# Macaron block on one core: FFN tiles turned by VectorE blocks and DMA instead of TensorE transposes, LayerNorm sums on ScalarE

## What is computed

```python
x = x + 0.5 * ffn(layernorm(x))
x = x + attention(layernorm(x))
x = x + 0.5 * ffn(layernorm(x))

def ffn(x):                       # T = 8192 tokens
    scores = sigmoid(x @ gate_w.T)
    idx = top_k(scores + gate_b, 4)
    w = scores[idx]; w = 2.5 * w / sum(w)       # comb: 16 weights a token, 12 of them zero
    y = sum over e of comb[:, e] * ((silu(g_e) * u_e) @ w2[e].T),  g_e, u_e = split(x @ w13[e].T)
    return y + the shared expert
```

## Time and profile before

| | us |
|---|---|
| median of 3 runs (833.62 to 835.65) | 834.15 |
| the profiled execution, whole | 834.31 |
| its span | 832.5 |
| TensorE busy | 819.8 (98%) |
| VectorE busy | 722.7 (87%) |
| ScalarE busy | 552.3 (66%) |
| GpSimd busy | 613.9 (74%) |

### The profile page before, as it was taken

How to read it: one execution, slowest core, us unless ns; L and a number is a source line. 1 busy time by engine, 2 the same in 40 slices (tenths; PEclk the granted TensorE clock), 3 DMA queues, 4 the chain that set the end, 5 groups by cost and what they waited for, 6 DMA issues and landing times.

```text
span 832.5 us, 16260 instructions
## 1 busy us (share of the span) xinstructions
PE 819.8 (98%) x4229; PEld 672.1 (81%) x4229; DVE 722.7 (87%) x2120; ACT 552.3 (66%) x1167; POOL 613.9 (74%) x559
## 2 busy tenths in 40 slices
PE   8899999999999999999999999999999999999998
PEld 7677777777777777899999989677777777777777
DVE  7989999999998987788888876799999999998886
ACT  5566666666666677776667666666666666666664
POOL 7767777777777688888888883476777777777664
PEclk9999999999999999999999999999999999999999
DMA  6787766666676633443333430555656655555553
GB/s 195 212 249 203 199 167 169 176 176 183 186 188 174 163 107 88 128 127 94 86 104 99 128 102 1 131 150 160 162 156 167 161 158 142 142 154 142 159 135 89
DMA packets 69376, 123.07 MB, mean 148 GB/s; under 512 B 8784, under 2 KB 19904, under 8 KB 69056
## 3 DMA queue, kind: packets, MB, share of 16 engines
q1 hardware_dynamic: 69312, 122.33, 54.7%
HBM read 104.28 MB, written 9.63 MB: 137 GB/s over the span
## 4 chain that ended last, share of the span: by engine, by line
PE 58%; DVE 3%; issue 1%; POOL 1%; DMA 1%; SPq 0%; ACT 0%; DVEq 0%; ACTq 0%; POOLq 0%
PE bank L1638 53%; PE bank L2009 4%; PE bank L1769 1%; DMA qkT<-comb_rows 1%; SPq L416 0%; DVE prob L1199 0%; POOL h_l L538 0%; DVE bank L1515 0%; PE bank L1746 0%; DVE xl L1482 0%; PE bank L1753 0%; DVE bank L1503 0%; POOL rstd L666 0%; DMA comb_rows<-combT 0%; DVE marked L1165 0%
## 5 line engine op out<-in xcount | busy, mean ns | idle before, releaser
L538 POOL TENSOR_TENSOR h_l<-probT,h_h 128x512 fp32r<-128x512 f32 x254 | 330.1, 1300 | 165.6 <-ACT h_h L760 164.7
L1638 PE MATMUL bank<-xh,w_h 128*128 128x512 f32 x545 | 223.4, 410 | 1.9 <-DVE prob L1199 1.7
L760 ACT ACTIVATE h_h<-probT 128x512 fp32r<-128x512 f32 (+1 forms) x285 | 178.7, 627 | 62.2 <-DVE probT L1209 59.5
L820 ACT ACTIVATE bank<-bank 128x512 f32<-128x512 f32 x252 | 146.8, 582 | 103.7 <-PE bank L1638 101.2
L1638 PE MATMUL bank<-xh,w_l 128*128 128x512 f32 x545 | 215.0, 395 | 0.0
L1638 PE MATMUL bank<-xl,w_h 128*128 128x512 f32 x545 | 214.8, 394 | 0.0
L1199 DVE TENSOR_TENSOR prob<-bank,qkT 128x512 f32<-128x512 f32 x252 | 172.9, 686 | 25.2 <-ACT bank L820 18.7
L1209 DVE TENSOR_TENSOR probT<-prob,bank 128x512 f32<-128x512 f32 x255 | 172.1, 675 | 15.0 <-POOL h_l L538 3.5
L1638 PEld LDWEIGHTS bank<-xh,w_h 128*128 128x128 f32 x545 | 103.2, 189 | 30.4 <-DVE prob L1199 3.5
L1638 PEld LDWEIGHTS bank<-xh,w_l 128*128 128x128 f32 x545 | 102.4, 188 | 23.8
L1638 PEld LDWEIGHTS bank<-xl,w_h 128*128 128x128 f32 x545 | 102.8, 189 | 19.3
(11 more groups left out here) (144 smaller groups left out, 1309.9 us busy)
## 6 DMA issues: line engine op xcount, KB each, us to landing
qkT<-comb_rows SPq DMA_DIRECT2D x190, 256.0 KB, 5.3
qkT<-comb_rows SPq DMA_DIRECT2D x124, 128.0 KB, 3.0
rows<-comb_rows SPq DMA_DIRECT2D x28, 512.0 KB, 7.2
stage<-stage SPq DMA_DIRECT2D x64, 128.0 KB, 2.4
X<-in_x SPq DMA_DIRECT2D x16, 256.0 KB, 7.4
stage<-in_x_t SPq DMA_DIRECT2D x16, 256.0 KB, 7.3
x_t<-stage SPq DMA_DIRECT2D x16, 256.0 KB, 2.0
out_x_t<-stage SPq DMA_DIRECT2D x15, 256.0 KB, 2.0
```

What stands on the lines that cost most here:

```text
L538: nc.gpsimd.tensor_tensor(lo, f, hi.bitcast(F32), ALU.subtract).then_inc(done, 1)
L760: return nc.scalar.activation(dst, src, ACT.Copy)
L820: nc.scalar.activation(bank[:, G_BANK[g], :], bank[:, G_BANK[g], :], ACT.Silu).then_inc(silu_done, 1)
L1638: return nc.tensor.matmul(dst, lhsT, rhs, start=start, stop=stop)
```

## The change

1. **Turning.** Token n * 128 + a * 32 + r of a tile now stands in column a * 128 + n * 32 + r. Then four 32x32 block transposes of VectorE and a DMA that moves partition groups give the full turn. In the first FFN VectorE turns each tile (`ffn_turn`, one 128x512 instruction), four DMAs write it to DRAM (`write_x1_rows`) and one DMA per sequence reads it back (`load_x1_rows`). In the second FFN VectorE turns the tokens of tile t + 4 (`turn_x2`), four DMAs write and one reads (`write_x2`, `load_x2`). `ffn_y`, `ffn_xT` and ScalarE's copies are gone. Four of the turns of the second FFN are made in the last batches of attention.
2. **Routing.** VectorE turns the logits and comb itself, in one 128x128 instruction each. The chain from logits to comb is spread over one more step of the tile.
3. **Statistics.** ScalarE sums them for tile T + 4 in steps 4 to 7 of tile T, in eight activations with an accumulator; VectorE's `ffn_stats` and `ffn_mv` stay at the start and in attention only.
4. **Loads.** `mask`, `cos` and `sin` are read at tiles 10 to 12 of the first FFN instead of at its start. The loops on SyncE and ScalarE over the FFN's tiles are written out.
5. **Scores.** Row 4's 640 columns are computed as two halves of 320, in six matmuls of 320 columns.

Core of the diff:

```diff
+            def ffn_means(T, Tx, q, part, base):
+                act.wait_ge(mv_done, ln_count(T - 1, base))
+                for n in (2 * part, 2 * part + 1):
+                    x = row_block(Tx, n) if base else raw_block(Tx, n)
+                    ins = nc.scalar.activation(unused[:, n, :, :], x, ACT.Identity, scale=MEAN_SCALE, accum_out=mv[...])
+            def ffn_vars(T, Tx, q, part, base):      # the same with ACT.Square, bias=mean, accum_out=mv[...]
...
-                    if base:
-                        if j == 0 and ahead:
-                            ffn_xT(T + 2, turn + (c + 2) // RING, (c + 2) % RING)
-                    elif j == PAIRS - 1 and not first:
-                        ffn_X(T - 1, T - 1)
+                    if j >= NB and j < PAIRS and (t is None or t + TURN_AHEAD < TILES):
+                        if j == NB and not base:
+                            act.wait_ge(x_next[q], 16 * (2 * turn + c // 2 + 1))
+                        (ffn_means if j < NB + 2 else ffn_vars)(T + TURN_AHEAD, T + TURN_AHEAD - base, q, j % 2, base)
...
+                nc.vector.transpose(logits[:], logitsT[:]).then_inc(logits_ready, 1)
+                nc.vector.transpose(combT[q][:], comb[:].rearrange("p n e -> p (n e)")).then_inc(combT_done, 1)
+                nc.vector.transpose(turned[c % 2], xT[c]).then_inc(turn_done, 1)
+                nc.vector.transpose(dst, X[:, tile_blocks(T), :].rearrange("p n d -> p (n d)")).then_inc(turn_done, 1)
...
+                for T in range(2, TILES):                      # SyncE, first FFN
                     store_x1(T - 2, (T - 2) % RING)
                     comb_rows(T, T % 2, 0, 0, T + 2 < TILES, 0 if T == TILES - 1 else None)
                     if T + 4 < TILES:
                         load_x(T + 4, T % 2)
                     if T + 2 < TILES:
-                        sp.wait_ge(y_ready, T - 1)
+                        sp.wait_ge(turn_done, T - 1)
                         load_xT(T + 2, (T + 2) % RING, (T + 2) // RING)
+                    if T == 10:
+                        load(mask[:], mask_d, rope_loaded)     # T == 11: cos, T == 12: sin
+                    if T >= 10:
+                        load_x1_rows(T - 10)
+                    write_x1_rows(T - 2, T % 2)
...
-                    k0, k1 = 512 * c, min(512 * (c + 1), (i + 1) * P)
+                    k0, k1 = wide * c, min(wide * (c + 1), (i + 1) * P)     # wide: 320 for row 4
```

447 lines of the change are left out of this document (255 added, 192 removed).

## The result

The changed kernel takes 867.03 us (median of 4 runs, 864.31 to 868.04), the kernel before on the same chip 834.03: a ratio of 1.039, 95% interval 1.0378 to 1.0403. I had forecast 825.8 us and a range of 813 to 840. So the change makes the kernel 4% slower, and the forecast has the wrong sign and misses by 41 us. The profiled execution took 868.0 us, its span is 866.3.

The account below looks back on a forecast made before the run. TensorE, busy 98%, was taken to bound the kernel before, loops through DRAM the changed one. From 834.3 us, -7.0 (second FFN), +0.8 (first FFN) and -2.3 (attention) gave 825.8 us, range 813 to 840.

Parts of the forecast that it names:

- the loop: Factors' path from VectorE through DRAM to VectorE: 18.64 us a turn, setting the second FFN's tiles, -7.0 us there.

Follow-up runs that it names:

- e16: Changed kernel with plain comb and turned-row writes, X and parameters loaded earlier, VectorE's step 5 weighting and comb moved ahead of the residual: 853.33 us.
- e19: As e16, but SyncE issues the previous tile's store between comb's write and its reads, not ahead of the write: 833.74 us, ratio 0.999.
- e13: Changed kernel with plain comb and turned-row writes, X and parameters loaded earlier, VectorE's comb and its turn ahead of residual and step 5's weighting: 844.33 us.
- e15: Changed kernel with VectorE's order of e13 alone; scattered writes, X and parameters as they are: 857.74 us, ratio 1.0273.

## What to carry to other kernels

When a change alters a DMA's shape (partitions, number of dimensions, distance of rows), its old duration is no row for the new one, even if it carries the same data: give it a range of its own, above all where a loop without slack runs through it. The profile of the write itself, and how much of the 16 DMA engines it keeps busy, then tells more than its size. Before moving a step in an engine's order, list what waits for it on the DMA queue: a store that waits for that step holds up every write behind it (19.6 us here, e16 against e19). After each such move, look at the waits: in e13 and e15 the loop had opened, and another wait had taken its place. And an engine that is busy 94% of a tile, with hand-overs at its ends, may already be the one that sets it.

## What the runs showed of the hardware

- A write of 128 partitions of 512 bytes to 128 consecutive rows lands about as fast as one of 72 (1.54 us against 1.46, and 1.8 to 1.9 for both with a store just ahead); the same bytes in a three-dimensional pattern with rows 2 KB apart take 2.40 to 2.5 us, 0.51 instead of 0.33 of it to issue, and keep the 16 DMA engines busy to 0.26 while they move, where the plain write reaches 0.9.
- Four writes of 64 KB in such patterns are issued over 4.9 to 7.0 us in most tiles of the first FFN and over 2.9 to 4.1 in the second, and the next store takes up to 2.86 us to issue; one write of the same 256 KB with 2 KB rows is issued in 0.41.
- A turn of 32x128 on VectorE lasts as long (0.30 us) as one of 128x128.
- After its 4.26 us gap TensorE starts the changed kernel's matmul at 29.83 with 0.80 us where 0.39 to 0.50 is usual:

```profile
29.83 0.80 PE L1792 MATMUL bank<-xh,w_h 128*128 128x512 f32 x1 [4.26 <-DVE prob L1308]
```

The matmuls behind it start 0.43 us apart until 34.26 and 0.23 apart again from 34.55. The granted clock from 30 to 35 us is 0.56, so for most of that stretch it is the 1.2 GHz level (0.86 over 20 to 45 us), where the kernel before, with a gap of 1.67 us at this place, kept 1.00. The eleven steps from 29.83 to 34.55 take 4.72 us, where eleven of 0.23 would be 2.5, so this gap costs about 2 us more than its own length.
